# Batch 1's attention inputs made earlier, key rows on another DMA queue, two buffer clears on another engine

## The reference

```python
x = x + mamba_and_moe(layernorm(x))          # 8 experts, top 2
x = x + ffn(layernorm(x))                    # 128 -> 384 -> 128
x = x + attention(layernorm(x))              # below
x = x + ffn(layernorm(x))

c_kv   = x @ W_dkv.T
q      = (x @ W_dq.T @ W_uq.T).reshape(B, T, 16, 8)
q_lat  = einsum('bqhd,hdl->bhql', q, k_eff)
attn   = softmax(where(causal, einsum('bhql,bkl->bhqk', q_lat, c_kv) / sqrt(8), -inf))
y      = einsum('bhql,hld->bqhd', einsum('bhqk,bkl->bhql', attn, c_kv), v_eff)
```

## Time and profile before

| | us |
|---|---|
| median of 3 runs | 796.23 (795.66 to 796.41) |
| profiled execution | 794.94 |
| its span | 793.2 |
| PE busy | 652.0 (82%) |
| DVE busy | 544.9 (69%) |
| ACT busy | 380.8 (48%) |
| POOL busy | 311.2 (39%) |
| transfers of SP's queue (q1) | 25.45 MB |

### The profile page before, as it was taken

One profiled execution on the slowest core, in us unless ns is written; L12 is line 12 of the kernel. 1 busy time (PEld: TensorE's weight loads), 2 busy tenths in 40 slices (PEclk: granted clock), 3 DMA queues, 4 the chain that ended last, 5 costly groups with the idle time before them and its releaser, 6 DMA issues.

```text
span 793.2 us, 10922 instructions
## 1 busy us (share of the span) xinstructions
PE 652.0 (82%) x3316; PEld 341.1 (43%) x3335; DVE 544.9 (69%) x1361; ACT 380.8 (48%) x606; POOL 311.2 (39%) x273
## 2 busy tenths in 40 slices
PE   1957888879268888778999999964999598998897
PEld 1413333344023333256666666732545244444355
DVE  6779999975999999843523554368587486686042
ACT  1556666615436666424554444411256365566721
POOL 5237676600369996312667332452202012101010
PEclk9968999999569999999999999985999899999999
DMA  6900000000300000020132200541404303300001
GB/s 154 336 0 2 0 0 1 0 1 0 106 4 21 17 15 0 0 78 17 41 88 70 75 14 14 85 98 28 74 11 54 50 3 53 43 4 2 2 14 40
DMA packets 31673, 32.06 MB, mean 40 GB/s; under 512 B 5394, under 2 KB 26914, under 8 KB 31362
## 3 DMA queue, kind: packets, MB, share of 16 engines
q1 hardware_dynamic: 26274, 25.45, 14.2%
q0 software_dynamic: 2496, 5.15, 2.1%
q10 hardware_dynamic: 2848, 0.78, 0.5%
HBM read 13.90 MB, written 9.25 MB: 29 GB/s over the span
## 4 chain that ended last, share of the span: by engine, by line
PE 42%; DVE 6%; ACT 3%; issue 3%; DMA 3%; ACTq 1%; POOL 0%; DVEq 0%; POOLq 0%
PE ps L1414 37%; DVE arena L1335 3%; PE ps L1596 2%; DMA arena<-arena 2%; ACT arena L959 2%; PE ps L1692 1%; ACTq L951 1%; PE ps L1581 1%; DVE stats L1034 1%; DVE x L1275 1%; PE ps L1699 0%; DVE nb L1047 0%; ACT arena L948 0%; ACT arena L967 0%; DMA arena<-moe_rows 0%
## 5 line engine op out<-in xcount | busy, mean ns | idle before, releaser
L1414 PE MATMUL ps<-arena 128*128 (+12 forms) x2003 | 410.5, 392 | 108.7 <-DVE arena L1210 38.4
L1414 PEld LDWEIGHTS ps<-arena 128*128 128x128 bf16 (+3 forms) x2022 | 173.7, 136 | 289.8 <-DVE arena L1210 87.3
L746 POOL TENSOR_TENSOR arena<-arena 128x1024 f32<-128x1024 f32 x64 | 150.6, 2359 | 50.7 <-ACT arena L897 46.7
L1203 DVE TENSOR_TENSOR_SCAN arena<-ps,arena 128x512 f32<-128x512 f32 x128 | 149.3, 1208 | 5.7 <-ACT ps L902 3.2
L1335 DVE CUSTOM_DVE_ANT_0 arena<-ps,cmask 128x128 f32<-128x128 f32 (+3 forms) x256 | 115.8, 520 | 34.2 <-PE ps L1414 27.8
L1414 PE MATMUL ps<-arena,ident 128*128 128x512 f32 x256 | 123.5, 604 | 0.2
L959 ACT ACTIVATE arena<-ps 128x1024 f32<-128x1024 f32 (+3 forms) x128 | 85.0, 709 | 62.7 <-PE ps L1414 55.6
L897 ACT COPY arena<-ps 128x1024 f32<-128x1024 f32 x64 | 64.8, 1012 | 79.2 <-PE ps L1414 71.5
L902 ACT ACTIVATE ps<-arena 128x512 f32<-128x512 f32 x128 | 84.3, 690 | 13.6 <-DVE arena L1203 13.4
L732 POOL DMA_INDIRECT moe_out<-arena,xT x46 | 45.0, 979 | 89.7 <-DVE arena L1359 85.4
L1387 DVE TENSOR_TENSOR arena<-arena,ps 128x512 f32<-128x512 f32 x46 | 31.7, 689 | 70.2 <-PE ps L1414 55.8
(11 more groups left out here) (181 smaller groups left out, 636.9 us busy)
## 6 DMA issues: line engine op xcount, KB each, us to landing
arena<-arena SPq DMA_DIRECT2D x120, 64.0 KB
moe_rows<-arena SPq DMA_DIRECT2D x2, 1495.0 KB, 14.5
arena<-moe_rows SPq DMA_DIRECT2D x8, 325.0 KB, 4.8
arena<-in_L_attn_a_Wu SPq DMA_DIRECT2D x1, 2048.0 KB, 8.7
arena<-in_L_attn_a_Wg SPq DMA_DIRECT2D x1, 2048.0 KB, 8.2
arena<-moe_out SPq DMA_DIRECT2D x4, 512.0 KB, 4.2
x<-n_L_attn_a_hidden_states SPq DMA_DIRECT2D x4, 256.0 KB, 5.1
out<-x SPq DMA_DIRECT2D x4, 256.0 KB, 2.3
```

The costliest lines, as they stand in the source:

```text
L746: G.tensor_tensor(dBx[:, g % RING, :], dx[:, e, :], bs[:, g % 2, :], ALU.mult).then_inc(s_dbx, 1)
L1203: V.tensor_tensor_scan(hst[:, g % 2, cs], bank(6 + c), dBx[:, g % RING, cs], 0.0, ALU.mult, ALU.add).then_inc(s_scan, 1)
L1414: return T.matmul(o, l, rr, start=start, stop=stop)
```

## The change

Four things are different.

1. `norm`, `normalise`, `turn` and the query half of `qk` of batch 1 leave the ramp for blocks 37 to 45 of the block loop. To make room, the FFN steps of batches 0 and 1 come one to seven blocks earlier. The key half of batch 1 stays in the ramp, at its very start.
2. The 14 key DMAs of each batch are issued by POOL (`place_keys`, `first_keys`) instead of SP. SP keeps the 14 query DMAs.
3. The key buffers of batches 1 and 2 are cleared by a copy on ACT (`clear`) instead of a memset on POOL.
4. The last value buffer is cleared in block 39 instead of after the loop.

```diff
+        Q_PARTS, K_PARTS = (0, 0, 1, 0, 2, 1, 1), (0, 1, 0, 2, 0, 1, 2)
-        ramp = {(1, 1): [("combine", 2), ("f_norm", 0, 2)], (2, 0): [("f_normalise", 0, 2), ("f_turn", 0, 2)],
+        ramp = {(0, 0): [("clear", 1), ("qk", 1, 1)], (0, 1): [("qk_rest", 1, 1)], (1, 0): [("vals", 1)], (1, 1): [("combine", 2), ("f_norm", 0, 2)], (2, 0): [("f_normalise", 0, 2), ("f_turn", 0, 2)],
...
-                (3, 1): [("tile", 2, 1), ("f_turn", 0, 3)], (4, 0): [("tile", 2, 2)], (4, 1): [("tile", 3, 0), ("f_down", 2)],
+                (3, 1): [("clear", 2), ("tile", 2, 1), ("f_turn", 0, 3)], (4, 0): [("tile", 2, 2)], (4, 1): [("tile", 3, 0), ("f_down", 2)],
...
-            for n in range(1, NB):
-                if a == max(0, PAIRS * n - 10):
+            for n in range(2, NB):
+                if a == (6, 14)[n - 2]:
...
-                  34: [("f_down", 0)], 35: [("f_add", 0), ("norm", 0)], 36: [("normalise", 0)], 37: [("turn", 0)],
-                  38: [("qk", 0, 0)], 39: [("qk_rest", 0, 0)], 40: [("qk", 0, 1)], 41: [("qk_rest", 0, 1)], 42: [("vals", 0)],
-                  43: [("f_down", 1)], 44: [("f_add", 1)]}
+                  32: [("f_down", 0)], 33: [("f_add", 0), ("norm", 0)], 34: [("normalise", 0)], 35: [("turn", 0)],
+                  36: [("f_down", 1)], 37: [("f_add", 1), ("norm", 1)], 38: [("qk", 0, 0), ("normalise", 1)],
+                  39: [("qk_rest", 0, 0)], 40: [("qk", 0, 1)], 41: [("qk_rest", 0, 1)], 42: [("vals", 0)],
+                  43: [("turn", 1)], 44: [("qk", 1, 0)], 45: [("qk_rest", 1, 0)]}
...
-        tile_after = {30: (0, 0), 31: (0, 1), 32: (0, 2), 34: (1, 0), 35: (1, 1), 36: (1, 2)}
+        tile_after = {29: (0, 0), 30: (0, 1), 31: (0, 2), 33: (1, 0), 34: (1, 1), 35: (1, 2)}
...
             load_outputs(2)
             load_outputs(3)
+            place_ones(1)
+            place_zeros(1)
             attend(parts, steps)
...
+            def place_keys(b, parts):
+                for n, part in enumerate(K_PARTS):
+                    if part in parts:
+                        for r in range(2):
+                            rows = slice(64 * r + HS * n, 64 * r + HS * n + HS)
+                            pool.dma_start(kz[rows, kslot(b), r, :, :],
+                                           qp[64 * r:64 * r + 64, 1, part, :]).then_inc(s_qk[b][1], 16)
+
+            def first_keys(b, w):
+                if w:
+                    if b >= SL:
+                        pool.wait_ge(s_s2, 2 * UNITS * (b - SL + 1))
+                    pool.wait_ge(s_kz, min(b, SL - 1) + 1)
+                    pool.wait_ge(s_qh, 2 * b + 2)
+                    place_keys(b, (0,))
...
                 G.tensor_tensor(qp[:, w, 2, :], qr[:, w, :], qp[:, w, 1, :], ALU.subtract).then_inc(s_qp, 1)
+                if w:
+                    pool.wait_ge(s_qp, 2 * n + 2)
+                    place_keys(b, (1, 2))
...
+                if i == 39:
+                    pool.wait_ge(s_fd, 2)
+                    clear_values(NB - 1)
...
-            pool.wait_ge(s_fd, 2)
-            clear_values(NB - 1)
-            pool.wait_ge(s_hT, 2 * NBLK)
-            clear_keys(1)
-            attend(parts, ramp_first)
-            pool.wait_ge(s_cb, NB)
-            clear_keys(2)
-            attend(parts, steps[len(ramp_first):] + last_ffn)
+            attend(parts, steps + last_ffn)
...
+            def clear_keys(b):
+                if b == 1:
+                    act.wait_ge(s_dn, 2 * NBLK)
+                else:
+                    act.wait_ge(s_cb, NB)
+                S.copy(kz[:, kslot(b), :, :, :].rearrange("p r j l -> p (r j l)").bitcast(F32).rearrange(
+                    "p (n l) -> p n l", l=L // 2),
+                       zeror[:, :].bitcast(F32).unsqueeze(1).to_broadcast([P, 2 * PAIRS, L // 2])).then_inc(s_kz, 1)
```

More of the change, by code:

```diff
@@ L524, in build @@
                   1: [("h2turn", 0), ("targets", 0)], 22: [("targets", 1)],
-                  27: [("combine", 0), ("f_norm", 0, 0)], 28: [("f_normalise", 0, 0)], 29: [("f_turn", 0, 0)],
-                  30: [("combine", 1), ("f_norm", 0, 1)], 31: [("f_normalise", 0, 1)], 33: [("f_turn", 0, 1)],
-                  34: [("f_down", 0)], 35: [("f_add", 0), ("norm", 0)], 36: [("normalise", 0)], 37: [("turn", 0)],
-                  38: [("qk", 0, 0)], 39: [("qk_rest", 0, 0)], 40: [("qk", 0, 1)], 41: [("qk_rest", 0, 1)], 42: [("vals", 0)],
-                  43: [("f_down", 1)], 44: [("f_add", 1)]}
-        ramp_first = steps[:steps.index(("qk_rest", 1, 0))]
-        tile_after = {30: (0, 0), 31: (0, 1), 32: (0, 2), 34: (1, 0), 35: (1, 1), 36: (1, 2)}
+                  26: [("combine", 0), ("f_norm", 0, 0)], 27: [("f_normalise", 0, 0)],
+                  28: [("f_turn", 0, 0), ("combine", 1), ("f_norm", 0, 1)], 29: [("f_normalise", 0, 1)], 30: [("f_turn", 0, 1)],
+                  32: [("f_down", 0)], 33: [("f_add", 0), ("norm", 0)], 34: [("normalise", 0)], 35: [("turn", 0)],
[3 more added lines that the diff above has]
+        tile_after = {29: (0, 0), 30: (0, 1), 31: (0, 2), 33: (1, 0), 34: (1, 1), 35: (1, 2)}
         items = []
@@ L623, in place_zeros, with place @@
                                  ).then_inc(s_qz[b], 16)
-            def place(b, w, parts):
-                g = kslot(b) if w else b % SL
-                for n, part in enumerate(((0, 0, 1, 0, 2, 1, 1), (0, 1, 0, 2, 0, 1, 2))[w]):
+            def place(b, parts):
+                for n, part in enumerate(Q_PARTS):
                     if part in parts:
@@ L631, in place @@
                             rows = slice(64 * r + HS * n, 64 * r + HS * n + HS)
-                            sp.dma_start(kz[rows, g, r, :, :] if w else qq[rows, g, :, :],
-                                         qp[64 * r:64 * r + 64, w, part, :]).then_inc(s_qk[b][w], 16)
+                            sp.dma_start(qq[rows, b % SL, :, :],
+                                         qp[64 * r:64 * r + 64, 0, part, :]).then_inc(s_qk[b][0], 16)
             def place_first(b, w):
+                if w:
+                    return
                 if b >= SL:
                     sp.wait_ge(s_s2, 2 * UNITS * (b - SL + 1))
-                if w == 0 and b:
+                if b > 1:
                     if b < SL:
@@ L641, in place_first @@
                     place_zeros(b)
-                sp.wait_ge(s_qh, 2 * b + w + 1)
-                place(b, w, (0,))
+                sp.wait_ge(s_qh, 2 * b + 1)
+                place(b, (0,))
             def place_rest(b, w):
-                sp.wait_ge(s_qp, 2 * (2 * b + w) + 2)
-                place(b, w, (1, 2))
+                if w:
+                    return
+                sp.wait_ge(s_qp, 4 * b + 2)
+                place(b, (1, 2))
             place_ones(0)
@@ L751, in _, with clear_first_keys @@
                 powers(2 * TB * h, 2 * TB)
-            def clear_keys(b):
-                G.memset(kz[:, kslot(b), :, :, :].rearrange("p r j l -> p (r j l)").bitcast(F32), 0.0).then_inc(s_kz, 1)
+            def clear_first_keys():
+                G.memset(kz[:, kslot(0), :, :, :].rearrange("p r j l -> p (r j l)").bitcast(F32), 0.0).then_inc(s_kz, 1)
             def clear_values(b):
@@ L793, in split_max @@
                 G.tensor_tensor(third, rest, second, ALU.subtract).then_inc(s_m3, 1)
-            parts = dict(norm=norm, f_norm=lambda p, b: norm(b), qk_rest=split_qk, split_max=split_max,
+            parts = dict(norm=norm, f_norm=lambda p, b: norm(b), qk=first_keys, qk_rest=split_qk, split_max=split_max,
                          o_add=add_output)
@@ L805, in _ @@
                     pool.wait_ge(s_wpc, NPREP)
-                    clear_keys(0)
+                    clear_first_keys()
                 if 20 <= i < 20 + NB - 1:
                     clear_values(i - 20)
+                if i == 39:
+                    pool.wait_ge(s_fd, 2)
+                    clear_values(NB - 1)
                 attend(parts, in_moe.get(i, []))
@@ L971, in f_turn @@
                 S.copy(ffn_input(p, b), bank(7)).then_inc(s_fxT, 1)
-            parts = dict(f_turn=f_turn, turn=turn, qk=first_part, vals=vals, place_max=place_max, scores=exps, values=outputs,
+            def clear_keys(b):
[6 more added lines that the diff above has]
+                       zeror[:, :].bitcast(F32).unsqueeze(1).to_broadcast([P, 2 * PAIRS, L // 2])).then_inc(s_kz, 1)
+            parts = dict(f_turn=f_turn, turn=turn, clear=clear_keys, qk=first_part, vals=vals, place_max=place_max, scores=exps, values=outputs,
                          h2turn=lambda c: moe_input(HB + c), route=lambda: logits(1), top_a=lambda: router_exp(1), prep=prep_copies)
```

1 line of the change is left out of this document (added).

## The result

The changed kernel takes 799.02 us against 795.81 for the kernel before, timed side by side: a ratio of 1.0043, with a 95% interval from 1.0024 to 1.0063. A second timing gave 1.0044 (1.0024 to 1.0065). I had forecast 794.0, slightly faster; it is slower by some 3.4 us. It lies inside the stated range only because that range spans two values of the pitch, the time from one of POOL's DMAs to the next, and neither of them came.

What follows compares the result with a forecast made beforehand. It took DVE to bound the ramp, and PE the steady stage except for two stalls on max-row DMAs. +0.2 - 4.4 + 2.0 = -2.2 us gave 792.7 profiled, 794.0 at the median; range 785 to 806.5.

Steps and rivals of the forecast that it cites:

- the pitch: POOL's queue: time from one plain DMA to the next, taken as 0.96 us, between ends of 0.66 and 1.26.
- POOL issues like SP: Rival, faster: POOL issues a plain DMA every 0.66 us, as SP does; sum -11.4, 784.8 us; chance 0.15.
- Block loop and ramp, +0.2: Everything up to the attention: loop +1.4 for PE's added work, ramp and loop together +0.2 us.
- first combine: Ramp: it moves from 537.76 to 539.3 us, waiting for SP's later fetch of batch 2's outputs.
- power: Ramp: POOL's power for the layernorm comes after batch 1's key DMAs, at 547.9 plus 1.0 us, instead of 541.67.
- the FFN tile's silu product: End of the ramp: gate, silu and product give 558.8 us against 559.67, -0.9.
- the ring of four buffers costs DVE nothing: Block loop: DVE does not wait for block-output buffers at 0.96 us per POOL DMA; first maxima begin at 527.2 us.
- First stall, -4.4: Steady stage: PE waits for POOL's split, not for a DMA, and goes on at 622.8 instead of 627.2 us.
- the rival on slowed queries: Steady stage and ramp: POOL's key transfers load SP's eight engines and slow the queries; +2, 798.2 us; chance 0.13.
- Second stall, +2.0: Steady stage: ACT issues later, at 669.8 and 670.5; its max-row DMA lands at 676.2 us instead of 674.24.
- The signs: Wrong if: combine before 538, pitch near 1; max rows over 5 us to land at 622; SP under 60 KB per us.
- ACT's clears: Ramp: no DVE instruction takes 3 us any more; a clear takes ACT 4.0 us, holding its next silu by +1.1.

Runs made afterwards that it cites:

- after_again: The changed kernel timed and profiled once more, against the kernel before: 799.57 us, ratio 1.0044.
- late_keys_sp: The changed kernel with the key rows of batches 2 and 3 placed by SP's queue again: 794.52 us, 0.9981 of the kernel before.
- first_keys_sp: The changed kernel with the keys of batch 0 alone placed by SP: 800.21 us, 1.0057 of the kernel before.
- batch_3_keys_sp: The changed kernel with the keys of batch 3 alone placed by SP: 789.25 us, 0.9934 of the kernel before.
- batch_2_keys_sp: The changed kernel with the keys of batch 2 alone placed by SP: 802.17 us, 1.0071 of the kernel before.
- clears_alone: The kernel before with one edit, ACT instead of POOL clears the key buffers of batches 1 and 2: 795.85 us, 0.9990 of the kernel before.
- queries_pool_too: The changed kernel with the queries of batches 2 and 3 placed by POOL too: 803.87 us, 1.0112 of the kernel before.

## Why the prediction was wrong, point by point

**The pitch.** Taken as 0.96 us, bounded by 0.66 and 1.26, measured 0.56 to 0.57. It was named the one unknown on which all turned. The indirect DMAs of the same engine, the nearest rows, still take 0.98 in the same trace, so their 1.26 said nothing of plain ones. The pieces that I had compared, 128 and 64, were counted from the shapes; POOL's queue moved 2496 packets for its 78 indirect DMAs, 32 each, and 5184 - 2496 = 2688 for the 56 plain ones, 48 each. The sum with the measured pitch would have been further off, so the pitch is not what failed: the rival "POOL issues like SP" has its condition met and its 784.8 us missed by 14.

**Block loop and ramp, +0.2.** Measured from the first block output on: -3.0 us in this profile, -2.7 in that of after_again, -1.3 in that of late_keys_sp, whose median says -0.0019, -1.5 us with an interval through zero. The forecast was too high here by 1.5 to 3.2 us. The single steps seem to hold, but by luck: first combine 538.84 (forecast 539.3), power 544.71 behind the keys of batch 1 (547.9 at my pitch), second combine 549.85 (551.4), the FFN tile's silu product 558.58 (558.8). Without the 2.1 us that this execution lost ahead of the block loop each comes 2.3 to 5.3 us before its forecast. The first combine did not wait for its fetch either, which was my reason for it; in after_again it did, by 1.53 us at 537.74. ACT's clear took 3.61 us (4.0). One statement was wrong: "the ring of four buffers costs DVE nothing". The outputs were issued in time, but the one issued at 522.01 needed 6.08 us to land, behind and beside the keys, and DVE waited 1.84 us for its buffer; the first maxima began at 530.17 instead of 527.2, 0.9 late without the 2.1. Whether that costs the kernel anything is open, since first_keys_sp, which removes the wait, delays the first scores and the fetch instead.

**First stall, -4.4.** Measured -4.05 at its end, of which -0.9 was there before: -3.2, and -3.7 in the median of batch_3_keys_sp. Here 2.1 us of it are given back at a low clock, in batch_3_keys_sp 0.1. The size nearly holds, the reason does not. I had the DMA landing 2.3 us after a late issue at 620.4 and PE waiting for POOL's split. The split was 0.9 us later than before, ACT issued at 616.13, 0.9 earlier, and its DMA took 7.06 us to land. Two thirds of the wait stayed, just as the rival on slowed queries had it. That it is the slowed queries alone is argued: from 616 to 620 us SP's queue moved only 0.07 MB more and POOL's 0.23, SP's nearly ceased at 619, and the max rows moved from 620 to 622, when POOL's had ended too.

**Second stall, +2.0: the term that failed.** I let SP's 14 queries go "at 65 KB per us", through at 673.0, as if POOL's keys moved beside them for nothing, and made the late split (ACT's issue at 670.5, 3.4 us later than before) the reason for what loss there was. Measured: +6.3 us at its end (from -1.96 to +4.34), and +7.2 in the median of batch_2_keys_sp. Of the 6.3, 1.3 are PE's wait for the split, less than half of what I gave it. The other 5.0 are the landing, 12.03 us in place of 7.11, which I had expected to get shorter: the queries moved 0.27 MB in 7 us, 39 KB per us, not 65. The 1.65 us of low clock behind it are this execution's alone.

The step behind it is the count of what stands in front. In the kernel before ACT issued at 667.13, when SP, at 0.66 us each from 658.95, had issued 12 or 13 of its 28 DMAs: the queries. The keys came after the max row and did not delay it. Moving them to POOL took nothing out of the line in front, and put them beside it. At the first stall ACT issued last at 617.02, behind 27 of 28, and there the move took half the line away. I had written the argument for one stall and carried it over to the other.

**The signs.** I had written that I am wrong if the max rows still take over 5 us to land at 622, or if SP's transfers are slower than 60 KB per us. Both came: 7.06 us, and 39 KB per us.

**The rival.** "The key transfers slow the queries" had the mechanism and 798.2 us, closest to the 799.0, with a chance of 0.13. That its number came so close is luck. Its price left the second stall out altogether: it kept the forecast's +2.0 there, 4 to 5 us too little, and the forecast's +0.2 for loop and ramp, 1.5 to 3.2 us too much, and the two cancel in part. That the keys slow the queries is measured: SP's queue moved 0.27 MB beside POOL's 0.35 where it had moved 0.51 alone. The rival's condition, that both queues load the same eight engines, is not: no view names the engines, and the load of the two queues from 661 to 668 us adds up to 69.2% of sixteen. What I held against the rival, that SP is half as often in front of ACT, was true of only one of the two stalls.

**ACT's clears.** The 3.5 us instructions of DVE went as forecast. The gain did not go into a wait for the fetch in clears_alone: its profile has 1.7 us of it at the start of the attention, and its median shows none that can be told from zero.

## What to carry to other kernels

Before a transfer is moved to another queue, count what stands in front of the DMA that is waited for at the moment of its issue; in this kernel only what was in front was saved (10.21 us became 7.06), and what was moved beside it slowed it (7.11 became 12.03). Where a small transfer is waited for, issuing the large ones at another time can be worth more than any choice of queue: here 0.983 against 1.004. Here the DMAs that POOL issued were work of 0.56 us each in its program: a power behind eight of them held DVE up for 3.0 us, and what other engines need belongs in front of them. And before stages of two profiles are compared, find the first place where the kernels differ and set both to zero there: 2.1 of the 6.0 us between these two had nothing to do with the change.

## What the runs showed of the hardware that I had not expected

- A plain DMA of 64 KB took POOL 0.56 us, an indirect one 0.98 with 1.26 from one to the next, SP's plain one 0.66.
- Key transfers ran at 0.42 MB / 4 us = 105 KB per us from POOL's queue alone, in packets of 4 KB, and at 0.98 / 14 = 70 from SP's alone, in packets of 1 KB; both queues together moved 0.62 MB in 7 us, 89 KB per us, less than POOL's alone.
- A DMA of ACT landed after 12.03 us behind 14 transfers of SP with POOL's beside them, and was waited for by nobody when SP's moved an eighth of their bytes, POOL's as many as before (issued at 670.31, its packets moved from 671.6 to 671.9). In queries_pool_too nobody waited for it either, but there POOL's transfers were through before ACT issued.
- Beside a POOL memset of 128x4096 a 128x4 instruction of DVE took 3.45 us, and 0.17 without it. ACT's copy of the same size (526.97 to 530.58 in clears_alone) ran beside DVE's maxima, which kept their 0.29 and 0.55 us.
- The clock after a stall of PE is not a fixed price: behind waits of 7.06 and 6.92 us at the same place it was 0.50 for 8 us in one execution (623 to 631) and 1.00 in another; behind 12.03 and 11.97 us the first was at 0.50 until past 686, 8 us on, and the other for 4.
- Executions of kernels that are the same up to the first block output reached it up to 2.8 us apart (355.6 to 358.4 us).
